# The keys' rotation in the last causal attention: two groups' rotations move from GpSimd to VectorE

## The reference

```python
def _L3_attn_ref(X, W_KQV, W_O):
    def _rope(x, freqs):
        xr = x[..., ::2]
        xi = x[..., 1::2]
        cos = jnp.cos(freqs)
        sin = jnp.sin(freqs)
        yr = xr * cos - xi * sin
        yi = xr * sin + xi * cos
        return jnp.stack([yr, yi], axis=-1).reshape(x.shape)
    KQV = jnp.einsum('bsd,ed->bse', X, W_KQV)
    K, Q, V = jnp.split(KQV, [D, 2 * D], axis=-1)
    K, Q, V = (to_heads(K), to_heads(Q), to_heads(V))
    Q = _rope(Q, freqs)
    K = _rope(K, freqs)
    scores = jnp.einsum('bhqd,bhkd->bhqk', Q, K) / sqrt(d)
    scores = jnp.where(causal, -jnp.inf, scores)
    probs = jax.nn.softmax(scores, axis=-1)
    heads = jnp.einsum('bhqk,bhkd->bhqd', probs, V)
    return jnp.einsum('bsd,ed->bse', acts, W_O)
```

## Time and profile before

| | us |
|---|---|
| median of 3 runs | 748.72 (747.66 to 748.99) |
| the profiled execution | 747.51 |
| its span | 745.7 |
| TensorE matmul busy | 597.0 (80% of the span) |
| VectorE busy | 474.7 (64%) |
| ScalarE busy | 249.3 (33%) |
| GpSimd busy | 119.3 (16%) |
| mean granted clock of TensorE | 0.887 of full |

### The profile page before, as it was taken

The page is one execution under the profiler, slowest core; times in us unless marked ns, Lnnn a source line. Parts: engine busy times, 40 slices in busy tenths (PEclk is TensorE's granted clock), DMA queues, the critical chain, the costliest instruction groups (busy, mean ns, idle before and its releaser), DMA issues.

```text
span 745.7 us, 10768 instructions
## 1 busy us (share of the span) xinstructions
PE 597.0 (80%) x4297; PEld 391.0 (52%) x4297; DVE 474.7 (64%) x1212; ACT 249.3 (33%) x371; POOL 119.3 (16%) x118
## 2 busy tenths in 40 slices
PE   1414599977899889969987679999779958998567
PEld 1314255667455646556765646456435654556425
DVE  7788867677587567754344634875554455876585
ACT  2342124415334333424323342344221022443261
POOL 5022611013220041000002014100200043102020
PEclk9657579979899999997998899999799986999879
DMA  9700000000000000000000000000000000000000
GB/s 298 304 0 1 0 1 1 2 1 2 0 1 2 1 1 2 1 1 1 1 0 1 1 0 1 1 2 1 1 0 1 0 1 0 2 1 1 1 0 29
DMA packets 6721, 12.41 MB, mean 17 GB/s; under 512 B 528, under 2 KB 4880, under 8 KB 6288
## 3 DMA queue, kind: packets, MB, share of 16 engines
q1 hardware_dynamic: 6672, 11.73, 4.4%
HBM read 11.21 MB, written 0.52 MB: 16 GB/s over the span
## 4 chain that ended last, share of the span: by engine, by line
PE 69%; DVE 23%; POOL 4%; ACT 2%; issue 2%; DVEq 0%; ACTq 0%; POOLq 0%
PE ps L413 52%; PE ps L476 11%; PE ps L429 3%; DVE st L1121 2%; PE ps L495 2%; DVE xn L1309 2%; POOL rs L327 2%; DVE mx L1220 2%; DVE big L1226 2%; DVE mv L1124 1%; DVE x L1239 1%; PE ps L585 1%; ACT big L876 1%; DVE big L1451 1%; DVE s L1449 1%
## 5 line engine op out<-in xcount | busy, mean ns | idle before, releaser
L1220 DVE TENSOR_REDUCE mx<-ps 128x8 f32<-128x1024 f32 x80 | 98.0, 1224 | 58.8 <-PE ps L413 58.7
L876 ACT ACTIVATE big<-ps 128x1024 f32<-128x1024 f32 x80 | 81.9, 1024 | 129.3 <-PE ps L476 129.3
L1226 DVE TENSOR_TENSOR big<-ps,mx 128x1024 f32<-128x1024 f32 x80 | 98.0, 1225 | 6.9
L476 PE MATMUL ps<-kt,big 128*128 128x128 f32 x640 | 90.9, 287 | 7.0 <-DVE big L1226 6.9
L413 PE MATMUL ps<-KTm,qk 32*128 32x512 f32 x320 | 95.6, 677 | 0.0
L327 POOL TENSOR_TENSOR rs<-ve,negh 128x4 f32<-128x4 f32 x26 | 26.6, 1024 | 411.7 <-DVE ve L1126 411.6
L476 PEld LDWEIGHTS ps<-kt,big 128*128 128x128 f32 x640 | 71.4, 145 | 35.0 <-DVE big L1226 18.5
L413 PE MATMUL ps<-xnT,wt 128*128 128x512 f32 (+1 forms) x148 | 78.8, 672 | 3.1 <-DVE big L1496 3.1
L413 PEld LDWEIGHTS ps<-wt,big 128*128 128x128 f32 (+1 forms) x480 | 56.0, 191 | 9.2 <-issue 9.1
L413 PE MATMUL ps<-wt,big 128*128 128x128 f32 (+1 forms) x480 | 59.8, 279 | 0.0
L413 PEld LDWEIGHTS ps<-big,vaug 128*32 128x32 f32 x1280 | 30.4, 109 | 48.0 <-ACT big L876 45.5
(11 more groups left out here) (273 smaller groups left out, 783.4 us busy)
## 6 DMA issues: line engine op xcount, KB each, us to landing
wt<-in_weights SPq DMA_DIRECT2D x1, 1664.0 KB, 17.0
wt<-in_weights SPq DMA_DIRECT2D x1, 1603.0 KB, 11.9
wt<-in_weights SPq DMA_DIRECT2D x6, 256.0 KB, 11.2
bt<-in_bconsts SPq DMA_DIRECT2D x1, 1024.0 KB, 8.5
rowt<-in_rows SPq DMA_DIRECT2D x1, 975.0 KB, 6.6
wt<-in_weights SPq DMA_DIRECT2D x1, 832.0 KB, 13.5
wt<-in_weights SPq DMA_DIRECT2D x1, 608.0 KB, 18.0
wt<-in_weights SPq DMA_DIRECT2D x1, 580.0 KB, 5.5
```

What stands on the lines that cost most here:

```text
L476: ins = pe.transpose(heads_of(pair(g, u))[:, j // HG, j % HG, :], pr[:, (u % 2) * HH + j, :], ident)
L876: act.activation(half, heads_of(pair(g, u)), ACT.Exp, scale=SCALES[l]).then_inc(*s.step(f"exp{u}"))
L1220: dve.tensor_reduce(top, S, AX.X, ALU.max).then_inc(*s.step())
L1226: dve.tensor_tensor(pr[:, half * HH:(half + 1) * HH, :].rearrange("p (i j) k -> p i j k", i=2), S, top.unsqueeze(3).to_broadcast([P, 2, HG ...
```

## The change

In L3a, GpSimd's `rotate_keys` is no longer called, ScalarE no longer copies raw k out of `bank(1)`, and VectorE rotates k straight from `bank(1)` into `td`, right after the q of the same group, with the same helper and tables. The name of the step, `krot`, is kept, so TensorE's wait in phase 8 now names a VectorE step. In VectorE's phase 6 the order becomes q and k of group 0, then q and k of group 1. L0x is untouched.

```diff
@@ GpSimd, program(g)
-                if l in ("L0x", "L3a"):
+                if l == "L0x":
                     yield from rotate_keys(n, l)
@@ ScalarE, program(g)
                     if l == "L3a":
-                        read(t.ta[:, GB:2 * GB, :], four(bank(1)), "k", "kraw")
                         values()
@@ VectorE, program(g)
                     dve.wait_ge(*s.at("L3a.q"))
                     rotate(bank(0).rearrange("p (h d) -> p h d", d=HD), const("c3"), const("s3"), tc, "qrot", "pair")
+                    dve.wait_ge(*s.at("L3a.k"))
+                    rotate(bank(1).rearrange("p (h d) -> p h d", d=HD), const("c3"), const("s3"), td, "krot", "pair")
```

## The result

The changed kernel took 739.79 us (median of 4 runs, 736.89 to 742.16), the kernel before 748.19 us (4 runs, 746.02 to 748.99). The ratio is 0.989, with a 95% interval of 0.984 to 0.994. Forecast were 740.5 us in a range of 738.4 to 746.5. The profiled execution of the changed kernel took 742.16 us, the slowest of the four, its span 740.4 us.

What follows compares the result with a forecast made beforehand. The prediction took TensorE's wait for GpSimd's key rotations in L3a, and the slow clock after it, as the bound. 3.1 us of wait, less 0.1 contention, plus 5.2 of clock made 8.2 us: 740.5 us, range 738.4 to 746.5.

Steps and rivals of the forecast that it cites:

- The bound: In L3a, TensorE waits for GpSimd's key rotations; moving them to VectorE turns group 1's keys 3.1 us earlier.
- VectorE's price: In L3a, each new key rotation on VectorE takes 2.08 us; contention with GpSimd costs 0.1 us, bounds 0 and 0.4.
- The rival that VectorE would become slow beside GpSimd: In L3a, VectorE's four rotations become the bound at up to 4.20 us each, giving 754.0 us; chance 0.03.
- The removed copy: In L3a, dropping ScalarE's raw key copies gains nothing more, since its next work still waits for TensorE's v.
- The covers: In L3a, TensorE's masks and first scores hide VectorE's spreading of both groups' keys, group 1's with 0.6 us to spare.
- The clock term: At L3a's attention start, TensorE runs at clock 1.00 instead of 0.50, saving 5.16 us from first mask to values.
- The argument for the clock's level: Ahead of L3a's attention, a 1.5 us idle gap with dense work on both sides leaves TensorE's clock at 1.00.
- Downstream: Behind L3a, clock falls in L3x and L3f may shift; zero taken as the middle, 2 us at most either way.
- The total: Whole kernel: 3.1 us of wait, less 0.1 contention, plus 5.2 for the clock, 8.2 us gained; chance 0.62.
- The cold one: In L3a the clock falls anyway, so only the wait of 3.0 us goes, giving 745.7 us; chance 0.28.

Runs made afterwards that it cites:

- e3: Changed kernel, but in L3a GpSimd rotates group 0's keys and VectorE only group 1's; 743.52 us, ratio 0.9942.
- e2: Kernel before, with 24 idle transposes on TensorE in L3a ahead of its wait for GpSimd's group 1 keys; 742.82 us, ratio 0.9936.
- e4: Changed kernel, with VectorE rotating group 1's keys twice, so TensorE idles longer ahead of their turn; 747.72 us, ratio 1.000.
- e5: Changed kernel, with 10 idle transposes on TensorE in L3a between the turns of group 1's q and keys; 741.64 us, ratio 0.9933.
- e7: Changed kernel, with 32 idle transposes in L0x's 7.8 us gap and ten in L3a's remaining gap; 742.01 us, ratio 0.9889.
- e11: Changed kernel, with 26 idle transposes on TensorE in the softmax gap of L3x; 736.87 us, ratio 0.9885.
- e6: Changed kernel, but in L3a VectorE rotates only group 0's keys and GpSimd group 1's; 745.61 us, ratio 0.9996.
- e8: Kernel before, run again without edit for a second profile; 746.62 us.

## Why the prediction was right

- **The bound.** GpSimd's rotation was what ended last, and VectorE's four rotations have taken its place in the chain, ending 3.0 us sooner. Forecast 3.1 less 0.1.
- **VectorE's price.** 2.1 us for each rotation, as the row of the old one said. The addition beside GpSimd took 0.74 in place of 0.69 us, within the bounds of 0 and 0.4. The rival that VectorE would become slow beside GpSimd did not come about: all four took 2.1 us. GpSimd's spreading (614.93 to 615.97) lies beside part of one rotation only. In e3, where GpSimd began its spreading just ahead of VectorE's, the price was real, 1.5 us for 0.69. The Trainium skill, GPSIMD Engine Reference, § 1. Specifications, names VectorE instructions with two SBUF inputs as those that contend, and the instruction of e3 is of that kind.
- **The removed copy.** Nothing, as said: ScalarE idled 3.74 us ahead of the values instead.
- **The covers held.** Group 0's first scores started 0.5 us behind the mask as in L1a, with VectorE's spreading at 616.55 in time; group 1's was in time as well.
- **The clock term.** 5.16 forecast, 5.19 measured by itself in e2. It was the right mechanism at the right size against the profile at hand. Against the second profile of before it is 3.6, since there the clock came back sooner, and in e4 a fall cost 2.2. The step leaned on one execution, and on one of a rarer kind.
- **The argument for the clock's level** was right in its outcome and incomplete in its reason. I compared the longest gaps (1.5 us here, 1.73 in L1x, 1.36 in L3x) and the busy time around them. In e3 it fell with more busy time and a gap of 1.02 us at most. Nine profiled executions kept it in L3a, six with the gap at 1.5 to 1.6 us and three with a filled one (e2, e5, e7); why e3's masks and scores were not enough is open. The Trainium skill, TensorE: Matmul & The Clock Gate, Part 1, says that the judging runs free of the kernel, so that moments vary from run to run. The two profiles of before agree as far as the moment goes, 13.6 and 9.8 us to the return behind the same code. Within L3a's projections it hardly varied: the return came 9.4 to 9.6 us behind the first statistics in all fourteen profiles.
- **Downstream.** I took zero, with 2 us either way. It was a loss of 0.4 us against the first profile of before and of 2.4 against the second, the latter beyond my bound. The stretches show where it lies: L3x and L3f now meet the clock at another moment, with 20.5 us at 0.50 in all where it had been 17 or 13.7. This is the term that was mis-sized; filling L3x's gap in e11 gains 2.7 us there.
- **The total.** 8.2 or 6.7 us won and 0.4 or 2.4 given back make 7.8 or 4.3 us by stages. By the ratios the three comparisons gave 8.2 us (0.989), 5.5 (0.9926) and 8.2 (0.9891), each uncertain by 2 to 4 us, with the differences "ahead" in them. The medians of all runs, 747.1 of before (77 runs) and 741.6 of the changed kernel (19), are 5.5 us apart. That the first comparison met the forecast gain of 8.2 us so closely is luck in part.
- **The rivals.** The cold one (745.7), a fall with the wait gone, did not come about in any profile of the changed kernel. That e6's median, 745.6, equals it is chance: e6 kept a wait of 2.63 us, and its start took 14.0 us from mask to values and not 17.1.

Open: what parts the heaps at 737 and 742. Between the three profiles of the changed kernel the whole difference lies ahead of L3a, and over all profiles "ahead" runs from 597.2 us (e11, a run of 736.3) to 602.6 (e6). But the shortest of these with the changed kernel's other stages would give an execution of about 739.2 us (597.2 + 28.8 + 47.9 + 23.35 + 40.2, and 1.8 more than the span), so "ahead" as seen here does not reach 737 by itself.

## What to carry to other kernels

Price a wait of TensorE twice: its length, and what the engine does at half clock afterwards; the second was the larger here, 5.2 of 8.2 us against one profile and 3.6 of 6.7 against the other. Take that price from a stage of the same kernel that runs the same instructions at the other level, and test it by filling the gap and leaving the wait. And when a change moves the rest of the program in time, expect that clock falls further on move as well, so compare two profiles of each kernel by stages before an effect under 3 us is believed.

## What the runs showed of the hardware that was not expected

- The granted clock fell with TensorE busy 2.48 of the last 3.50 us, on masks and 32-row scores, and no gap over 1.02 us (e3). It stayed with TensorE busy 1.70 of 3.50 us and a gap of 1.51 us (changed kernel).
- In the attention's start the clock came back 7.6 (e4), 9.8 (e8) and 13.6 us (before) behind the first mask, with TensorE busy nearly without a break. Ahead of it, in the turns and projections of the same L3a, it came back at 607.3, 5.8 us after they began at 601.5 (before).
- Of a spreading of keys on VectorE and one on GpSimd at the same time, the one that started second was the long one: VectorE's 1.5 us instead of 0.69, with GpSimd 0.02 us ahead (e3); GpSimd's 1.54 instead of 1.04, with VectorE 0.04 us ahead (changed kernel).
- The same code ahead of L3a took between 597.2 and 602.6 us.
